# Scores in longer runs between fewer weighings, halved maxima of one reduction in four, and late value tiles spread

## The chip, the cores and the metric

One core of a Trainium2 chip. The time is the device time of one execution in microseconds; lower is better.

## The reference

Four sequences of 1024 tokens with 256 channels. A layer norm, attention with 16 heads of 16 dimensions and rotary positions, a layer norm and a residual; then a layer norm, a mixture of 8 experts (each token goes to 2), a layer norm and a residual. What matters here is the attention:

```python
q = (x @ Wq.T + bq).reshape(B, T, H, D)   # k, v alike; q and k rotated
scores = jnp.einsum('bthd,bshd->bhts', q, k) / np.sqrt(D)
attn = jax.nn.softmax(scores, axis=-1)
out = jnp.einsum('bhts,bshd->bthd', attn, v).reshape(B, T, C)
```

The softmax of this kernel subtracts a row maximum, which has to be known before the exponentials, as the scores that are exponentiated have keys on the partitions.

## The kernel before

Each engine runs its own program, in the order in which it is written; counting semaphores join them. There is no scheduler: an instruction whose wait isn't met holds up all behind it on its engine.

**Setup.** ScalarE turns the q and k weights' columns into the order that the rotation wants (`w_turn`, `b_turn`), copies the four halves of the cosine and sine tables out of PSUM and the bias columns `b_c`. Then it normalises the first 512 tokens. TensorE turns the tables, then the bias columns, then the first tokens (`turn_x(0)`), and projects (`project`). VectorE applies the rotation (`rope_unit`), GpSimd a part of it, ScalarE splits the result in a high and a low part, and SyncE stores these and loads them again as "stacks", three of which hold q and k of a group of four heads each.

**Groups.** There are 16 groups of 4 heads (`NG`), a group in 16 units (`UNITS`). In one unit the loop does two things on TensorE. For a later group, it computes the scores of 128 queries against all 1024 keys for two heads (`max_scores`: head `a` in two halves of 512 keys, to banks 4, 5 for `a` = 0 and 6, 7 for `a` = 1); VectorE reduces both banks of a head in one instruction to a row maximum (`reduce_max`). For the present group, it computes the transposed scores of 128 keys against 512 queries for four heads (`scores`, three banks in turn), which ScalarE exponentiates into `pt`. A maximum beside a score is called a pair here; they use different rows of the array. The maxima run `LEAD` = 5 units ahead of a group's end.

**Weighing.** `weigh` multiplies the exponentials of the unit two before (`LAG`) with the values: four heads side by side in the columns of the array, into bank 3. It does this in two parts of 256 queries, one after every second pair. Twice a group the sum in bank 3 is complete, and ScalarE copies it out (`save_o`, line 1356); the first weighing of the next half waits for that.

**Maxima.** After 8 units of maxima GpSimd splits them in two parts (`split_max`), VectorE turns them (`turn`), and SyncE brings them into the stack by way of memory. GpSimd also copies the values of a later group (`copy_values`) and, in groups 9 and 13, scales the output of a batch (`norm_o`), all in one queue.

**Ahead of the loop.** The maxima of group 0 and of the first 5 units of group 1 are computed without scores beside them. Of the 16 value tiles (`project_v`), 4 are done with the projections, and the other 12 follow one by one behind the maxima of the first 12 units. The loop waits until all are saved.

## Time and profile before

| | us |
|---|---|
| median of the runs shown | 1600.58 |
| the runs | 1593.86, 1600.58, 1622.9 |
| the profiled execution | 1592.43 |
| its span in the profile | 1590.5 |

| engine | busy us | share of the span |
|---|---|---|
| TensorE (PE) | 1446.7 | 91% |
| VectorE (DVE) | 1107.6 | 70% |
| ScalarE (ACT) | 852.3 | 54% |
| GpSimd (POOL) | 427.4 | 27% |

A time of the profile is counted from the span's start. PE are matmuls, PEld the loads of their stationary operand, and a matmul record's end is modelled. The stages that the change touches lie in the first half: setup and projections up to 98, maxima ahead of the loop up to 155, the loop up to 811. Output projection and experts follow.

### The profile page before, as it was taken

How to read it: one execution, taken by the hardware profiler on the slowest of the kernel's cores; microseconds unless marked ns; L12 is line 12 of the kernel's file. 1: busy time of each engine (PE TensorE's matmuls, PEld its weight loads, DVE VectorE, ACT ScalarE, POOL GpSimd, SP SyncE). 2: the span in 40 equal slices, each digit the busy share in tenths (PEclk: the TensorE clock that was granted, in tenths of full speed). 3: DMA queues.
4: the chain of work that ended last, by engine and by line, in shares of the span. 5: the costliest groups of instructions: out<-in, count | busy, mean ns of one | idle time of the engine just before them, and what ended most of it. 6: DMA issues, size and time to landing. Idle time of an engine off the chain costs nothing.

```text
span 1590.5 us, 29998 instructions
## 1 busy us (share of the span) xinstructions
PE 1446.7 (91%) x9435; PEld 800.9 (50%) x9436; DVE 1107.6 (70%) x1978; ACT 852.3 (54%) x1624; POOL 427.4 (27%) x411
## 2 busy tenths in 40 slices
PE   7989999999999999999999438999999999999950
PEld 4444333333333333333355226777777777777740
DVE  5989899999999989999026774555555555455525
ACT  5531788888888878888865321222222222222215
POOL 3760000000000010001014143444444444444425
PEclk9997899999999999999999759999999999999985
DMA  5887146334545554550429623222212222121136
GB/s 171 241 254 129 44 98 169 65 71 81 88 82 89 100 88 64 82 89 16 158 54 213 225 98 91 33 33 33 31 32 33 33 33 33 33 33 31 32 85 199
DMA packets 125116, 141.80 MB, mean 89 GB/s; under 512 B 55131, under 2 KB 98949, under 8 KB 125030
## 3 DMA queue, kind: packets, MB, share of 16 engines
q1 hardware_dynamic: 109126, 121.98, 33.2%
q0 software_dynamic: 15904, 18.66, 7.2%
q8 instruction: 56, 0.92, 0.2%
q14 instruction: 30, 0.25, 0.1%
HBM read 86.30 MB, written 54.30 MB: 88 GB/s over the span
## 4 chain that ended last, share of the span: by engine, by line
PE 78%; DVE 7%; issue 5%; ACT 4%; DMA 2%; SPq 2%; POOL 1%; DVEq 0%; POOLq 0%; ACTq 0%
PE psum L1681 20%; PE psum L1528 18%; PE psum L1554 16%; PE psum L1700 11%; PE psum L1691 3%; PE psum L1509 2%; PE psum L1540 2%; PE psum L1612 1%; PE psum L1493 1%; ACT work L1346 1%; DVE mx L942 1%; ACT weights L1356 1%; PE psum L1667 1%; PE psum L1610 1%; DVE work L1141 1%
## 5 line engine op out<-in xcount | busy, mean ns | idle before, releaser
L942 DVE TENSOR_REDUCE mx<-psum 128x1 f32<-128x1024 f32 x512 | 622.9, 1222 | 29.2 <-PE psum L1528 26.3
L1346 ACT ACTIVATE work<-psum 128x512 f32<-128x512 f32 x1024 | 556.7, 597 | 106.1 <-PE psum L1540 43.8
L1528 PE MATMUL psum<-stack 48*128 48x512 f32 x1024 | 379.3, 457 | 6.7 <-DVE mx L942 6.0
L1540 PE MATMUL psum<-stack 50*128 50x512 f32 x1024 | 379.1, 450 | 0.0
L1681 PE MATMUL psum<-weights,values 128*128 x1136 | 341.1, 454 | 0.6 <-DVE values L1161 0.6
L1554 PE MATMUL psum<-work,values 128*32 128x256 f32 x4096 | 330.5, 395 | 9.2 <-ACT weights L1356 9.2
L1528 PEld LDWEIGHTS psum<-stack 48*128 48x128 f32 x1024 | 154.2, 191 | 221.7 <-DVE mx L942 184.7
L1681 PEld LDWEIGHTS psum<-weights,values 128*128 128x128 f32 x1136 | 211.8, 192 | 99.2 <-issue 3.1
L1423 ACT ACTIVATE values<-values 128x342 f32<-128x342 f32 x142 | 69.3, 488 | 250.1 <-DVE values L1173 250.1
L1700 PE MATMUL psum<-weights,work 114*128 (+1 forms) x852 | 198.7, 383 | 1.3 <-ACT work L1434 0.8
L1554 PEld LDWEIGHTS psum<-work,values 128*32 128x32 f32 x4096 | 82.5, 108 | 198.2 <-ACT work L1346 100.5
L1700 PEld LDWEIGHTS psum<-weights,work 114*128 114x128 f32 (+1 forms) x852 | 158.0, 192 | 21.3 <-issue 1.8
L1540 PEld LDWEIGHTS psum<-stack 50*128 50x128 f32 x1024 | 153.8, 188 | 17.3 <-ACT work L1346 17.3
L829 POOL DMA_INDIRECT values<-xn_d,at_x x71 | 70.0, 986 | 280.9 <-DVE at_w L1204 275.5
L1429 ACT ACTIVATE work<-psum,dots 128x256 f32<-128x256 f32 x71 | 33.6, 473 | 201.3 <-PE psum L1700 196.7
L1173 DVE TENSOR_TENSOR values<-psum,work 128x342 f32<-128x342 f32 x142 | 73.1, 515 | 92.0 <-PE psum L1681 68.1
L836 POOL DMA_INDIRECT y_d<-work,at_y x71 | 115.2, 1622 | 39.7 <-issue 27.2
L1176 DVE TENSOR_TENSOR values<-psum,work 128x342 f32<-128x342 f32 x142 | 73.1, 515 | 62.2 <-PE psum L1681 62.2
L1192 DVE COPY work<-psum 114x256 f32<-114x256 f32 x71 | 30.2, 425 | 118.2 <-PE psum L1691 118.2
L753 POOL CAST m<-mx 128x16 fp32r<-128x16 f32 x32 | 6.3, 197 | 376.4 <-DVE mx L942 376.4
L1181 DVE TENSOR_TENSOR values<-values 128x342 f32<-128x342 f32 x142 | 73.3, 516 | 14.7
L744 POOL TENSOR_TENSOR values<-weights,dots 128x512 f32<-128x512 f32 x16 | 20.5, 1283 | 225.4 <-issue 225.2
(184 smaller groups left out, 1190.6 us busy)
## 6 DMA issues: line engine op xcount, KB each, us to landing
stack<-qk_scr SPq DMA_DIRECT2D x192, 128.0 KB, 6.1
qk_scr<-weights SPq DMA_DIRECT2D x16, 1024.0 KB, 4.8
weights<-in_w SPq DMA_DIRECT2D x8, 1368.0 KB, 7.1
ot_scr<-weights SPq DMA_DIRECT2D x16, 512.0 KB, 3.2
weights<-in_w SPq DMA_DIRECT2D x8, 684.0 KB
work<-in_b SPq DMA_DIRECT2D x8, 684.0 KB, 8.8
y_d<-zeros SPq DMA_DIRECT2D x1, 4224.0 KB, 14.3
v_scr<-weights SPq DMA_DIRECT2D x32, 128.0 KB, 2.5
```

The costliest lines, as they stand in the source:

```text
L829: pool.indirect_dma_start(out=x_row, out_offset=None, in_=xn2_d, in_offset=bass.IndirectOffsetOnAxis(ap=at_x[:, 0:1], axis=0)).then_inc(s_ ...
L836: pool.indirect_dma_start(out=y_d, out_offset=bass.IndirectOffsetOnAxis(ap=at_y[:, 0:1], axis=0), in_=y_row, in_offset=None, compute_op=AL ...
L942: dve.tensor_reduce(mx[:, r, a, t:t + 1], bank(4 + 2 * a, 2), AX, ALU.max, negate=True).then_inc(s_max, 1)
L1173: dve.tensor_tensor(gates[c], bank(2 * c)[:, 0:CH], bias(0), ALU.add).then_inc(s_gb, 1)
L1176: dve.tensor_tensor(hid[:, CH * c:CH * (c + 1)], bank(2 * c + 1)[:, 0:CH], bias(HID), ALU.add).then_inc(s_ub, 1)
L1181: dve.tensor_tensor(hid[:, CH * c:CH * (c + 1)], hid[:, CH * c:CH * (c + 1)], gates[c], ALU.mult).then_inc(s_hid, 1)
L1346: act.activation(pt[u % 4][:, j, :], bank((c + HG * u + n) % 3), ACT.Exp, scale=SC).then_inc(s_exp, 1)
L1528: ins = pe.matmul(bank(4 + 2 * a + half), qs[t3][at:at + QROWS, r, P * t:P * (t + 1)], ks[t3][at:at + QROWS, r, 512 * half:512 * (half + 1 ...
L1540: pe.matmul(bank((t3 + HG * u + n) % 3), ks[t3][at:at + MROWS, r, P * st:P * (st + 1)], qs[t3][at:at + MROWS, r, 512 * half:512 * (half + ...
L1554: last = pe.matmul(bank(3)[32 * j:32 * (j + 1), at:at + 256], vg[p][:, st, j, :], pt[u % 4][:, j, at:at + 256], start=st + part == 0, stop ...
L1681: last = pe.matmul(dst, x_t[:, k, :], w1_sb[:, bass.ds(e, 1), k, col:col + CH].rearrange("p a n -> p (a n)"), start=k == 0, stop=k == KC - 1)
L1700: last = pe.matmul(bank(7)[:, 0:C], h_t[0:rows, k, :], w2_sb[0:rows, bass.ds(e, 1), k, :].rearrange("p a n -> p (a n)"), start=k == 0, sto ...
```

## The change

Between two weighings stand runs of three, three and two pairs, where there were two: `weigh` now takes any stretch of queries, and `weigh_pieces` gives per two units 384 queries, 128 of the same unit with 256 of the next one, and 256. Of an even unit the second head's maximum so falls on both sides of a weighing, and VectorE reduces its two halves by themselves (`mx_b` holds the second ones); `join_max` takes the smaller of the two negated values every 8 units, and GpSimd waits for that. `maxima` counts five reductions in two units. `LEAD` becomes 6. The 12 late value tiles are spread over the 16 + 6 units of maxima ahead of the loop, and SyncE's loads of the first maxima are put between its stores of values accordingly. In the setup, GpSimd reorders the weights in place of ScalarE, VectorE copies the tables and the bias columns, and TensorE turns the bias columns after the first tokens.

```diff
--- before.py
+++ after.py
@@ -35,7 +35,7 @@
 EARLY_V = 2
 UNITS = 2 * ST
 BLOCKS = HG * UNITS
-LEAD = 5
+LEAD = 6
 LAG = 2
 SC = D ** -0.5
 CH = HID // 2
@@ -88,6 +88,12 @@
 
     for g in range(NG):
         body(0, g)
+
+
+def maxima(g, m, a, half):
+
+    before = 5 * (UNITS * g + m) // 2 + m % 2
+    return before + (a + 1 if m % 2 or a == 0 else 2 + half)
 
 
 def settle(eng, passed):
@@ -584,9 +592,8 @@
             load_stacks(sp, 0, 1)
             for m in range(EARLY_V, NB):
                 store_v(sp, m)
-                if m == 5:
-                    load_max_rows(sp, 0, 0, 0)
-            load_max_rows(sp, 0, 0, 1)
+                if m in (3, 5):
+                    load_max_rows(sp, 0, 0, (m - 3) // 2)
             sp.wait_ge(s_ones, 3)
             load_stacks(sp, 0, 2)
             for parts_of in s_pst:
@@ -714,6 +721,15 @@
                 pool.wait_ge(s_pad, n + 1)
             pool.memset(cent_t[:, :, :], 0.0).then_inc(s_pad, 1)
 
+            pool.wait_ge(s_wqkv, 32)
+            for k in range(KC):
+                for i in range(2):
+                    pool.tensor_copy(w_turn[:, k, i, :, :].rearrange("p s (d h) -> p s d h", h=H),
+                                     w_qkv[:, k, C * i:C * (i + 1)].rearrange("p (h s d) -> p s d h", s=2, d=HALF)).then_inc(s_wp, 1)
+            for i in range(2):
+                pool.tensor_copy(b_turn[0:1, i, :, :].rearrange("p s (d h) -> p s d h", h=H),
+                                 b_row[0:1, C * i:C * (i + 1)].rearrange("p (h s d) -> p s d h", s=2, d=HALF)).then_inc(s_wp, 1)
+
             def rotate(w):
 
                 p = w % 2
@@ -747,7 +763,7 @@
             def split_max(g, r):
 
                 at = PAIRS * g + r
-                pool.wait_ge(s_max, 2 * UNITS * g + UNITS * (r + 1))
+                pool.wait_ge(s_cmb, at + 1)
                 after(pool, s_m2t, at)
                 settle(pool, passed_pool)
                 pool.tensor_copy(m2[:, :, 0, :], mx[:, r, :, :]).then_inc(s_mh, 1)
@@ -923,6 +939,11 @@
             stats(0)
             spread_tables()
             invert(0)
+            for n, (table, at) in enumerate(((cos_t, 0), (cos_t, 512), (sin_t, 0), (sin_t, 512))):
+                dve.wait_ge(s_tab, n + 1)
+                dve.tensor_copy(table[:, at:at + 512], bank(n)).then_inc(s_tabs, 1)
+            dve.wait_ge(s_bt, 1)
+            dve.tensor_copy(b_c[:, :], bank(6)[:, 0:4]).then_inc(s_bc, 1)
             stats(1)
             invert(1)
             for m in range(NB):
@@ -936,10 +957,21 @@
             def reduce_max(g, m, a):
 
                 r, t = m // ST, m % ST
-                dve.wait_ge(s_mp, 2 * (UNITS * g + m) + a + 1)
                 if t == 0 and a == 0:
                     after(dve, s_m2, PAIRS * (g - 1) + r + 1)
+                if m % 2 == 0 and a == 1:
+                    for half, dst in enumerate((mx[:, r, a, t:t + 1], mx_b[:, r, t // 2:t // 2 + 1])):
+                        dve.wait_ge(s_mp, maxima(g, m, a, half))
+                        dve.tensor_reduce(dst, bank(4 + 2 * a + half), AX, ALU.max, negate=True).then_inc(s_max, 1)
+                    return
+                dve.wait_ge(s_mp, maxima(g, m, a, 1))
                 dve.tensor_reduce(mx[:, r, a, t:t + 1], bank(4 + 2 * a, 2), AX, ALU.max, negate=True).then_inc(s_max, 1)
+
+            def join_max(g, r):
+
+                dve.wait_ge(s_max, maxima(g, ST * r + ST - 1, 1, 1))
+                both = mx[:, r, 1, :].rearrange("p (t s) -> p t s", s=2)[:, :, 0]
+                dve.tensor_tensor(both, both, mx_b[:, r, :], ALU.min).then_inc(s_cmb, 1)
 
             def turn(g, r):
 
@@ -956,6 +988,8 @@
                     if m == ST:
                         turn(g, 0)
                     reduce_max(g, m, 1)
+                    if m % ST == ST - 1:
+                        join_max(g, m // ST)
 
             def invert_sums(b):
 
@@ -1301,21 +1335,6 @@
                 act.activation(hl[w % 4][:, 0, :, :].bitcast(F32R), rr[w % 2], ACT.Copy).then_inc(s_hi, 1)
 
             deviation(0)
-            act.wait_ge(s_wqkv, 32)
-            for k in range(KC):
-                for i in range(2):
-                    act.activation(w_turn[:, k, i, :, :].rearrange("p s (d h) -> p s d h", h=H),
-                                   w_qkv[:, k, C * i:C * (i + 1)].rearrange("p (h s d) -> p s d h", s=2, d=HALF),
-                                   ACT.Copy).then_inc(s_wp, 1)
-            for i in range(2):
-                act.activation(b_turn[0:1, i, :, :].rearrange("p s (d h) -> p s d h", h=H),
-                               b_row[0:1, C * i:C * (i + 1)].rearrange("p (h s d) -> p s d h", s=2, d=HALF),
-                               ACT.Copy).then_inc(s_wp, 1)
-            for n, (table, at) in enumerate(((cos_t, 0), (cos_t, 512), (sin_t, 0), (sin_t, 512))):
-                act.wait_ge(s_tab, n + 1)
-                act.activation(table[:, at:at + 512], bank(n), ACT.Copy).then_inc(s_tabs, 1)
-            act.wait_ge(s_bt, 1)
-            act.activation(b_c[:, :], bank(6)[:, 0:4], ACT.Copy).then_inc(s_bc, 1)
             normalise(0)
             save_xt(0)
             deviation(1)
@@ -1468,12 +1487,6 @@
                     src = spread[n // 2][:, 4 * (n % 2) + a, :, :].rearrange("p d h -> p (d h)")
                     last = pe.transpose(bank(n)[:, P * a:P * (a + 1)], src, ident[:, :])
                 last.then_inc(s_tab, 1)
-            pe.wait_ge(s_wp, 6)
-            for i in range(2):
-                for s in range(2):
-                    last = pe.matmul(bank(6)[:, 2 * i + s:2 * i + s + 1], b_turn[0:1, i, s, :], ones_f[0:1, 0:1], start=True, stop=True)
-            last.then_inc(s_bt, 1)
-
             def turn_x(m):
                 pe.wait_ge(s_xn, TB * (m + 1))
                 for k in range(KC):
@@ -1511,6 +1524,12 @@
                 last.then_inc(s_vp, 1)
 
             turn_x(0)
+            pe.wait_ge(s_wp, 6)
+            for i in range(2):
+                for s in range(2):
+                    last = pe.matmul(bank(6)[:, 2 * i + s:2 * i + s + 1], b_turn[0:1, i, s, :], ones_f[0:1, 0:1], start=True, stop=True)
+            last.then_inc(s_bt, 1)
+
             for m in range(NB):
                 project(2 * m)
                 if m + 1 < NB:
@@ -1523,11 +1542,11 @@
             def max_scores(g, t3, m, a, half):
 
                 r, t, at = m // ST, m % ST, 64 * a
-                if half == 0:
-                    after(pe, s_max, 2 * (UNITS * g + m) + a - 1)
+                if half == 0 and (g, m) != (0, 0):
+                    pe.wait_ge(s_max, maxima(g, m - 1, a, 1) if m else maxima(g - 1, UNITS - 1, a, 1))
                 ins = pe.matmul(bank(4 + 2 * a + half), qs[t3][at:at + QROWS, r, P * t:P * (t + 1)],
                                 ks[t3][at:at + QROWS, r, 512 * half:512 * (half + 1)], start=True, stop=True)
-                if half == 1:
+                if half == 1 or (m % 2 == 0 and a == 1):
                     ins.then_inc(s_mp, 1)
 
             def scores(g, t3, u, n):
@@ -1540,22 +1559,31 @@
                 pe.matmul(bank((t3 + HG * u + n) % 3), ks[t3][at:at + MROWS, r, P * st:P * (st + 1)],
                           qs[t3][at:at + MROWS, r, 512 * half:512 * (half + 1)], start=True, stop=True).then_inc(s_sp, 1)
 
-            def weigh(g, p, u, part):
+            def weigh(g, p, u, lo, hi):
 
                 half, st = u // ST, u % ST
-                if part == 0:
+                if lo == 0:
                     pe.wait_ge(s_exp, BLOCKS * g + HG * (u + 1))
                     if st == 0:
                         if half == 0:
                             pe.wait_ge(s_vg, g + 1)
                         after(pe, s_oe, 2 * g + half)
-                at = 256 * part
                 for j in range(HG):
-                    last = pe.matmul(bank(3)[32 * j:32 * (j + 1), at:at + 256], vg[p][:, st, j, :],
-                                     pt[u % 4][:, j, at:at + 256], start=st + part == 0, stop=st + part == ST,
+                    last = pe.matmul(bank(3)[32 * j:32 * (j + 1), lo:hi], vg[p][:, st, j, :],
+                                     pt[u % 4][:, j, lo:hi], start=st + lo == 0, stop=(st, hi) == (ST - 1, 512),
                                      tile_position=(0, 32 * j))
-                if part == 1:
+                if hi == 512:
                     last.then_inc(s_pv, 1)
+
+            def weigh_pieces(g, p, u, n):
+
+                pieces = {(0, 2): ((0, 0, 384),), (1, 1): ((0, 384, 512), (1, 0, 256)), (1, 3): ((1, 256, 512),)}
+                first = u // 2 * 2 - LAG
+                if first < 0:
+                    g, p, first = g - 1, 1 - p, first + UNITS
+                if g >= 0:
+                    for step, lo, hi in pieces.get((u % 2, n), ()):
+                        weigh(g, p, first + step, lo, hi)
 
             def group(i, c):
                 g, p, t3 = over(i, c, 1), c % 2, c % 3
@@ -1569,11 +1597,7 @@
                         if more:
                             max_scores(g + ahead, (c + ahead) % 3, m, n // 2, n % 2)
                         scores(g, t3, u, n)
-                        if n % 2 == 1:
-                            if u >= LAG:
-                                weigh(g, p, u - LAG, n // 2)
-                            elif c > 0:
-                                weigh(g - 1, 1 - p, UNITS + u - LAG, n // 2)
+                        weigh_pieces(g, p, u, n)
 
             pe.wait_ge(s_xt, 2 * NB)
             pe.wait_ge(s_va, 2 * EARLY_V)
@@ -1582,24 +1606,24 @@
                 for m in range([UNITS, LEAD][g]):
                     for n in range(HG):
                         max_scores(g, g, m, n // 2, n % 2)
-                    b = 2 * EARLY_V + m
-                    if g == 0 and b < 2 * NB:
-                        if m == 0:
-                            pe.wait_ge(s_r1, NU)
-                            pe.wait_ge(s_x1, NU)
-                        project_v(b // 2, b % 2)
+                    unit = UNITS * g + m
+                    late = 2 * (NB - EARLY_V)
+                    if unit == 0:
+                        pe.wait_ge(s_r1, NU)
+                        pe.wait_ge(s_x1, NU)
+                    for b in range(late * unit // (UNITS + LEAD), late * (unit + 1) // (UNITS + LEAD)):
+                        project_v(EARLY_V + b // 2, b % 2)
             pe.wait_ge(s_va, 2 * NB)
             pe.wait_ge(s_pad, 2)
             groups(pe, group)
             for u in range(UNITS - LAG, UNITS):
-                for part in range(2):
-                    weigh(NG - 1, 1, u, part)
+                weigh(NG - 1, 1, u, 0, 512)
 
 
             pe.wait_ge(s_wo, 48)
             pe.wait_ge(s_oe, 2 * NG)
             pe.wait_ge(s_exp, BLOCKS * NG)
-            pe.wait_ge(s_max, 2 * UNITS * NG)
+            pe.wait_ge(s_max, maxima(NG - 1, UNITS - 1, 1, 1))
 
             def project_o(u):
                 pe.wait_ge(s_div, 2 * (u // 4) + u % 4 // 2 + 1)
```

## Rows read from the trace of the kernel before

**Rows 1.** The chain that ended last, by engine, from the page

```profile
PE 78%; DVE 7%; issue 5%; ACT 4%; DMA 2%; SPq 2%; POOL 1%; DVEq 0%; POOLq 0%; ACTq 0%
```

**Rows 2.** Timeline of TensorE, last group and its end (start us, us)

```profile
761.55 0.73 PE L1540 MATMUL psum<-stack 50*128 50x512 f32 x2
...
762.78 0.73 PE L1540 MATMUL psum<-stack 50*128 50x512 f32 x2
...
808.43 2.37 PE L1554 MATMUL psum<-work,values 128*32 128x256 f32 x40
```

**Rows 3.** Timeline of TensorE in the loop, around a saved bank

```profile
305.96 0.49 PE L1528 MATMUL psum<-stack 48*128 48x512 f32 x1
...
306.30 0.39 PE L1528 MATMUL psum<-stack 48*128 48x512 f32 x1
...
306.99 0.64 PE L1554 MATMUL psum<-work,values 128*32 128x256 f32 x8 [0.30 <-ACT weights L1356]
...
307.56 0.50 PE L1528 MATMUL psum<-stack 48*128 48x512 f32 x1
```

**Rows 4.** Timeline of VectorE in the loop, the last row at half clock

```profile
288.27 2.46 DVE L942 TENSOR_REDUCE mx<-psum 128x1 f32<-128x1024 f32 x2 [0.38 <-PE psum L1528]
...
290.77 17.18 DVE L942 TENSOR_REDUCE mx<-psum 128x1 f32<-128x1024 f32 x14
308.33 2.46 DVE L942 TENSOR_REDUCE mx<-psum 128x1 f32<-128x1024 f32 x2 [0.38 <-PE psum L1528]
...
582.00 1.23 DVE L942 TENSOR_REDUCE mx<-psum 128x1 f32<-128x1024 f32 x1 [0.93 <-PE psum L1528]
```

**Rows 5.** Timeline ahead of the loop, with value tiles, and the loop's first pair

```profile
98.36 2.35 DVE L942 TENSOR_REDUCE mx<-psum 128x1 f32<-128x1024 f32 x2
...
107.70 0.74 PE L1528 MATMUL psum<-stack 48*128 48x512 f32 x4
...
108.47 2.36 DVE L942 TENSOR_REDUCE mx<-psum 128x1 f32<-128x1024 f32 x2 [0.82 <-PE psum L1528]
...
110.29 1.31 PE L1528 MATMUL psum<-stack 48*128 48x512 f32 x4
...
113.46 0.74 PE L1528 MATMUL psum<-stack 48*128 48x512 f32 x4
...
155.36 0.79 PE L1540 MATMUL psum<-stack 50*128 50x512 f32 x1
```

**Rows 6.** Timeline ahead of the loop, without value tiles

```profile
134.20 9.50 DVE L942 TENSOR_REDUCE mx<-psum 128x1 f32<-128x1024 f32 x8 [0.33 <-PE psum L1528]
...
135.48 0.73 PE L1528 MATMUL psum<-stack 48*128 48x512 f32 x2 [0.83 <-DVE mx L942]
```

**Rows 7.** Timeline of the setup

```profile
7.45 3.65 PE L1469 MATMUL psum<-ident,work 128*128 128x128 f32 x16 [7.45 <-DVE work L897]
...
9.12 2.23 ACT L1307 ACTIVATE work<-work 128x256 f32<-128x256 f32 x4 [0.72 <-DMA work<-in_bqkv]
...
14.42 2.06 ACT L1281 ACTIVATE work<-weights,work 128x256 f32<-128x256 f32 x4
...
19.18 5.61 PE L1493 MATMUL psum<-weights,work 128*128 128x512 f32 x8 [0.69 <-ACT weights L1287]
```

**Rows 8.** Timeline of GpSimd and of VectorE at group 10's start

```profile
568.45 4.72 POOL L774 TENSOR_TENSOR weights<-weights 128x1024 f32<-128x1024 f32 x2
...
573.65 0.21 DVE L948 STREAM_TRANSPOSE m_t<-m 128x32 f32<-128x32 f32 x1 [1.88 <-POOL m L755]
```

**Rows 9.** Stretches: length, PE busy (records), granted clock as a share, DMA share, GB/s

```profile
136.00:140.00 4.00, 2.69 (x7) 0.89 0.98 215
...
156.00:172.00 16.00, 15.70 (x80) 0.50 0.31 47
...
576.00:584.00 8.00, 8.00 (x56) 0.57 0.88 121
...
742.00:746.00 4.00, 4.00 (x44) 1.00 0.04 8
```

2 lines of the change are left out of this document (added).

## The prediction

> **What bounds the kernel now.** I read the chain that ended last first: TensorE holds 78% of it [rows 1]. Then I read the timelines of the stages which the diff touches, and asked of each which wait ends last.
>
> In the attention loop a slot (two pairs of a maximum beside a score, then a weighing of 256 queries) costs TensorE 0.34 us to the second pair (306.30 - 305.96), 0.57 us from the weighing to the next pair (307.56 - 306.99) and 0.32 us between these two, the rest of 1.23 [rows 3]. In the last group, where no maxima are left and VectorE is idle, the slot is still 1.23 us [rows 2]. So TensorE sets this loop, though its waits are put down to VectorE: the released semaphore had long been there. VectorE's fourteen reductions of a stretch lie 1.23 us apart [rows 4], but left alone it starts one every 1.13 us, although each record is 1.22 us long, because the end of one overlaps the start of the next [rows 6]. After a reduction's end TensorE follows within 0.06 us [rows 6]. One stall is left: twice per group the first weighing waits until ScalarE has saved the output bank [rows 3], and TensorE loses 306.99 - 306.62 = 0.37 us [rows 3]. Hence a half group is 16 x 1.23 + 0.37 = 20.06 us, which is the distance of the two stalls in VectorE's rows, 308.33 - 288.27 [rows 4].
>
> Ahead of the loop, group 0's maxima with twelve late value tiles run at 5.76 us for two units (107.70 to 113.46), with VectorE idle for 0.82 us there [rows 5]. Without value tiles (from 134.20) VectorE sets the pace at 2 x 1.13 us a unit [rows 6]. During this the granted clock falls to half and stays there through the first slots of the loop [rows 9].
>
> **Setup.** ScalarE loses the four weight reorderings, the bias, four table copies and the bias column: it normalised the first tile at 14.42 and could do so from 9.12 on, where the first of these copies stands, or earlier [rows 7]. What is late next is TensorE: it turns tables until 7.45 + 3.65 = 11.10 [rows 7]. At that row's 0.23 us a record, eight transposes of x take 1.9 us and the bias matmuls, now behind them, another 1.9 us: the first projection starts at 14.9 instead of 19.18. GpSimd was idle then. Six copies of 256 elements at the rate of its 128x1024 product (4.72 / 2 / 1024 = 2.3 ns an element [rows 8]) are 3.6 us, done at 12.7, under the transposes. At twice that price they would end at 16.3 and the gain would shrink to 1 us. VectorE gets the table copies and, worse, a wait for the bias columns, behind which the second tile's statistics queue: they end near 17, its normalised rows near 20, just when TensorE wants them. I take -4.0 us, bounds -1 and -5.
>
> **Ahead of the loop.** Twelve tiles now go over 22 units, one in every second unit but for two neighbours at the middle and the end. Take a unit followed by a tile. When TensorE issues its second head's maximum, VectorE holds at most the rest of one reduction and this one: 1.13 - 0.15 + 2 x 0.60 = 2.2 us of work (0.15 us: the overlap and the reply; a reduction of 512 is estimated at 0.60 us, namely 1.13 less 512 columns at 1024 / 1.067 us, that is, the same start cost as a whole one). TensorE comes back with data after 0.66 + 1.93 + 0.77 = 3.36 us (the pairs, the tile, 110.29 - 107.70 - 0.66, and 0.73 us for fresh scores with their semaphore) [rows 5]. That leaves a hole of 1.18 us, in every couple of units: 3 x 1.13 + 2 x 0.60 + 1.18 = 5.77 us. That is what two tiles in a couple cost before [rows 5]: spreading them hides nothing, as each one blocks TensorE's queue for longer than two buffers last. Eleven couples are 63.4 us. Before, 12 units at 2.88 and 9 at 2.26 us made 55; from the first reduction (98.36) to the loop (155.36) it was 57.0 [rows 5]. With the same edges the change adds 6.3 us, one unit of it (2.3 us) taken over from the loop, where it was free. I bound the term by +2 and +9.
>
> **The loop.** Per two units it has eight pairs as before and the same 1024 queries of weighing, but three switches instead of four. Weighings in a row take 0.43 us per 256 queries (the forty records at the end last 2.37 us [rows 2]; four weighings and the last one's record of 0.64 us: 1.73 / 4). A slot's 1.23 us less 2 pairs at about 0.235 and 0.43 leaves 0.33 us for a switch. TensorE alone would so need 4.92 - 0.33 = 4.59 us. VectorE needs 3 x 1.13 + 2 x 0.60 = 4.59 us. Both look like a gain of 7%. But a dependency joins them. The first pair of an even unit's second head (the third pair of its unit) waits for the whole reduction of the odd unit before it, in every two units, and that maximum is ready late: the last one is issued in the third run. Count from that pair at 0: its start after a wait and the way to the weighing 0.42; 384 queries and the switch 0.57 + 0.21 = 0.78; the fourth maximum and the next two 0.34 + 0.235; then 0.32 + 0.78; 0.34 to the odd unit's last pair: 3.22. Scores there after 0.39 + 0.04, the reduction 1.22, the reply 0.06: 4.93 us. The old period is 4.92. So the switch that is saved is spent waiting at this pair; that sum doesn't depend on how a run's third pair is spaced (0.21 to 0.34), since the pair after a wait pays what the other saves.
>
> What remains: the stall of the saved bank goes, since the first weighing now comes one pair later and lies under this wait. Its cover is the wait itself; were the wait gone, a few tenths would come back. Two joins a group cost VectorE about 0.3 us each (end of its reduction, an operation of 4 elements, no overlap), and 0.03 us of it appears. A half group becomes 19.75 instead of 20.06 us: -0.3 x 29 = -8.7 us. The last 22 units have no maxima, and there the saved switch counts: -2.8 us.
>
> GpSimd's queue takes some of it back. With a lead of six, the maxima of the first half are due one unit earlier, but in two groups the same 4.72 us of output scaling stand ahead of their splitting [rows 8]. VectorE waited 1.88 us there. It would now wait 1.88 + 2.46 + 0.3 = 4.65 us, and one period is paced by that: +2.8 us twice, and the save stall that it used to cover in part, +6.2 us in all. The ordinary value copy ends in time. Sum of the loop: -8.7 - 2.8 + 6.2 = -5.3 us, between -10 and +15; the upper bound is from the weighing of 128 queries. No row shows one. It may cost 0.21 us (half of 256) or as much as 256 does, 0.43 us, if loading its weights binds. I take the half, since the records of 256 queries hide their loads with time to spare, and 0.1 us more would already be +11 us.
>
> **The clock.** Before, eight slots in 155 to 173 took 2.16 us (582.00 less the reduction before it, 0.93 + 1.23) instead of 1.23 [rows 4, 9]: 7.5 us. It fell where TensorE had 67% records for 4 us [rows 9]. With tiles to the end its share ahead of the loop is some 80%, so I expect the loop to start at full clock: -7.5 us, bounds 0 and -7.5. The two waits for GpSimd go the other way. An equal wait made the clock fall once (7 us near half clock, 3.0 us lost) and once not [rows 9]. I expect that waits two and a half times as long make it fall both times: +3 us.
> The Trainium skill, in "TensorE: Matmul & The Clock Gate" under "Part 1: The HAM clock gate", says that the default state is the throttled one and that activity releases it, so a pause of TensorE is paid again afterwards. By that rule both waits cost a fall, where the rows alone would allow none; the sum would be 6 us lower without it.
>
> **Sum.** -4.0 + 6.3 - 5.3 - 7.5 + 3 = -7.5 us on the profiled execution's 1592.4 us (span 1590.5, 1.9 around it): 1585. That execution lies 8 us under the median of the three runs shown and 1.4 under their lowest; for a median of undisturbed runs I add 3 us: 1588 us.
>
> **The rivals.**
> *The dependency is not last* (0.12). Were the wait of the even unit's second head always met in time, half groups would be 18.7 us: 29 x 1.1 = 32 us less, 1556 us. For it: both engines' own sums are 4.59. Against it: the row of 1.22 us and the position of the last maximum leave no room.
> *The clock falls ahead of the loop* (0.2). The new mixture of short maxima and one tile in two units comes after a pause of 4 us at about 95. If it holds TensorE at half clock, a tile takes 1.93 x 2.16 / 1.23 = 3.4 us: 12 x 1.5 = 18 us, and the 7.5 us are not saved: 1613 us; half of it gives 1600. It decides from the point at which half clock lasts beyond the second tile. This is the case slower than before.
> *The weighing of 128 queries binds* (0.13): +0.1 to +0.21 us in each of some 120 couples, 1600 to 1612 us.
> *The setup gains nothing* (0.05), as GpSimd's reordering is slow: 1592 us.
> The forecast itself has 0.5, with its own range 1575 to 1597.
>
> **How the numbers follow.** The range 1564 to 1612 leaves out most of the first rival and the far end of the second and third. About 2% is what can be told from no change. Faster by over 2% (under 1569 against the median shown) is the first rival and the forecast's lower tail: 0.16. Slower by over 2% needs two of the slow cases at once: 0.07. The rest is 0.77.
>
> **What would show it.** Slots of the loop: a couple of units at 4.93 us with a wait of some 0.35 us at the third pair of even units, put down to the reduction. Reductions of 512 of about 0.69 us. No wait for the saved bank. The loop starting near 157.5 (161.7 less the setup's 4). A couple ahead of it at 5.77 us with holes of about 1.2 us in VectorE. The transposes in groups 10 and 14 waiting 4 to 5 us for GpSimd. The first projection at 15. I am wrong above all if a couple of units takes 4.6 us, or if the clock is at half before the loop.

## The result and the profile after

The changed kernel takes 1614.4 us in the median of four runs (1613.31 to 1615.6), the kernel before 1599.5 beside it. Each kernel has some longer executions with a lower granted clock over the whole span; the medians here include them, the ratios don't. The ratio is 1.0105 with a 95% interval of 1.0077 to 1.0134: slower by 1%, and the interval does not reach 1, which would be no difference. Predicted were 1588 us, with 1564 to 1612 as the range. The profiled execution took 1614.05 us, with a span of 1612.1; of before these were 1592.43 and 1590.5. Of the change's stages I name four events and take the distances between them.

| from | to | before, us | after, us | difference | predicted |
|---|---|---|---|---|---|
| start of the span | first reduction | 98.36 | 93.07 | -5.3 | -4.0 |
| first reduction | loop's first pair | 57.0 | 84.8 | +27.8 | +6.3 |
| loop's first pair | last saved bank | 655.5 | 656.3 | +0.8 | -9.8 |
| last saved bank | end | 779.6 | 777.9 | -1.7 | 0 |

The second row holds more than the whole difference. The timeline of the changed kernel there, TensorE and VectorE (start us, us), beside [rows 5]:

```profile
93.07 1.22 DVE L968 TENSOR_REDUCE mx<-psum 128x1 f32<-128x1024 f32 x1
...
96.68 3.78 PE L1522 MATMUL psum<-work,weights 128*128 128x256 f32 x8
101.64 1.23 DVE L968 TENSOR_REDUCE mx<-psum 128x1 f32<-128x1024 f32 x1 [3.64 <-PE psum L1547]
...
109.80 1.23 DVE L968 TENSOR_REDUCE mx<-psum 128x1 f32<-128x1024 f32 x1 [3.20 <-PE psum L1547]
...
117.25 1.22 DVE L968 TENSOR_REDUCE mx<-psum 128x1 f32<-128x1024 f32 x1 [2.69 <-PE psum L1547]
...
177.84 0.49 PE L1559 MATMUL psum<-stack 50*128 50x512 f32 x1
```

A couple of units takes 8.2 us (101.64 to 109.80) and then 7.5 us, where the prediction had 5.77. The first spread tile takes 3.78 us for its eight records (four products, two records each), twice the 1.93 us that I had worked out, and VectorE stands idle for 2.7 to 3.6 us behind each tile, not for 1.18. The stretches of the changed kernel say why (length, PE busy and records, granted clock, DMA share, GB/s):

```profile
100.00:110.00 10.00, 8.46 (x22) 0.54 0.84 205
110.00:120.00 10.00, 6.68 (x19) 0.80 0.98 141
120.00:130.00 10.00, 8.62 (x19) 0.50 0.25 54
130.00:140.00 10.00, 8.94 (x30) 0.84 0.25 56
...
150.00:160.00 10.00, 8.06 (x23) 0.67 0.26 56
160.00:170.00 10.00, 7.46 (x18) 0.64 0.12 27
```

A share between 0.5 and 1 is a mean over both levels, 1.2 and 2.4 GHz. The clock goes up and falls again through the whole stage, and some 55 of its 84.8 us run at the lower level. The records' busy share, 67 to 89%, looks like the 80% I had counted on. But at the lower level a record lasts about twice as long (the tile of 3.78 us), so this share says little; the section on the steps reads it where the clock was full.

In the loop, TensorE's timeline shows a couple of units around the wait that the change adds (the pair of L1547 at 301.68 is the third of an even unit):

```profile
300.87 0.49 PE L1547 MATMUL psum<-stack 48*128 48x512 f32 x1
...
301.20 0.39 PE L1547 MATMUL psum<-stack 48*128 48x512 f32 x1
...
301.68 0.50 PE L1547 MATMUL psum<-stack 48*128 48x512 f32 x1
...
302.18 0.85 PE L1572 MATMUL psum<-work,values 128*32 128x384 f32 x8
...
303.31 0.39 PE L1547 MATMUL psum<-stack 48*128 48x512 f32 x1
...
303.54 0.39 PE L1547 MATMUL psum<-stack 48*128 48x512 f32 x1
...
303.86 0.86 PE L1572 MATMUL psum<-work,values 128*32 128x128 f32 x16
```

A third pair that waits for nothing follows after 0.23 us (303.54 - 303.31); this one follows after 0.48 us, as VectorE's reduction isn't through. The weighing of 128 queries and the 256 of the next unit are one row of sixteen products, 303.86 to 304.65, as long as the one of 384 queries. A couple of units comes to 4.95 us where VectorE has nothing but reductions to do; with its joins and transpositions the mean is 5.03 (a quarter of 20.10, below). No row of a weighing is put down to the saved bank any more.

VectorE's joins and GpSimd's work beside them, timelines of both, and the transposition of group 11's first maxima, at group 10's start:

```profile
306.15 1.28 POOL L760 TENSOR_TENSOR values<-weights,dots 128x512 f32<-128x512 f32 x1 [18.48 <-issue]
...
306.67 0.78 DVE L974 TENSOR_TENSOR mx<-mx,mx_b 128x4 f32<-128x4 f32 x1
...
327.01 0.17 DVE L974 TENSOR_TENSOR mx<-mx,mx_b 128x4 f32<-128x4 f32 x1
...
589.51 4.68 POOL L790 TENSOR_TENSOR weights<-weights 128x1024 f32<-128x1024 f32 x2
...
594.66 0.21 DVE L980 STREAM_TRANSPOSE m_t<-m 128x32 f32<-128x32 f32 x1 [3.95 <-POOL m L771]
```

The same operation on four elements a partition takes 0.17 us, or 0.78 us when GpSimd's copy of a group's values lies over it. It then ends at 307.45, just behind that copy (306.15 + 1.28 = 307.43): the join waits until the copy is over. ScalarE's save of bank 3 gives the length of a half group (its timeline):

```profile
286.30 0.60 ACT L1375 ACTIVATE weights<-psum 128x512 f32<-128x512 f32 x1
306.16 0.60 ACT L1375 ACTIVATE weights<-psum 128x512 f32<-128x512 f32 x1
326.50 0.60 ACT L1375 ACTIVATE weights<-psum 128x512 f32<-128x512 f32 x1
```

Halves of 19.86 and 20.34 us alternate, 20.10 in the mean: the long ones hold the long join. Before, each was 20.05. The two that hold GpSimd's scaling are 25.80 and 25.92 us. In the last units, where no maxima are left, a half is 18.67 us instead of 20.04.

And of the setup, the timeline beside [rows 7]:

```profile
8.97 2.08 ACT L1315 ACTIVATE work<-weights,work 128x256 f32<-128x256 f32 x4 [0.44 <-DVE work L906]
9.06 2.31 POOL L727 COPY work<-work 128x256 f32<-128x256 f32 x4 [3.73 <-DMA work<-in_bqkv]
...
14.23 3.70 PE L1506 MATMUL psum<-weights,work 128*128 128x512 f32 x8
```

### The profile page after: what moved, and what is told of

It is laid out like the page before. It is cut to its first block, busy times and chain, and to the rows that moved or that the text cites. A ratio compares the mean times of both kernels' runs of the same rounds, so it can differ in the third digit from the quotient of the medians.

```text
span 1612.1 us, 30126 instructions
## 1 busy us (share of the span) xinstructions
PE 1449.6 (90%) x9419; PEld 823.6 (51%) x9420; DVE 1117.0 (69%) x2143; ACT 835.2 (52%) x1613; POOL 431.2 (27%) x417
## 4 chain that ended last, share of the span: by engine, by line
PE 68%; DVE 20%; issue 7%; DMA 1%; POOL 1%; ACT 1%; SPq 1%; DVEq 0%; POOLq 0%; ACTq 0%
PE psum L1705 20%; DVE mx L968 12%; PE psum L1724 11%; PE psum L1547 10%; PE psum L1572 10%; PE psum L1559 4%; PE psum L1522 3%; PE psum L1715 3%; PE psum L1636 2%; PE psum L1634 1%; DVE mx_b L965 1%; DVE mx L965 1%; PE psum L1506 1%; PE psum L1691 1%; PE psum L1655 1%
## 5 line engine op out<-in xcount | busy, mean ns | idle before, releaser
L1365 ACT ACTIVATE work<-psum 128x512 f32<-128x512 f32 x1024 | 544.4, 600 | 98.0 <-PE psum L1559 73.7
L968 DVE TENSOR_REDUCE mx<-psum 128x1 f32<-128x1024 f32 x384 | 465.4, 1220 | 46.2 <-PE psum L1547 36.9
L1547 PE MATMUL psum<-stack 48*128 48x512 f32 x1024 | 380.6, 459 | 39.8 <-DVE mx L968 20.0
L1547 PEld LDWEIGHTS psum<-stack 48*128 48x128 f32 x1024 | 161.6, 191 | 283.5 <-issue 122.8
L1572 PE MATMUL psum<-work,values 128*32 128x384 f32 x4080 | 303.5, 393 | 0.3
L1559 PEld LDWEIGHTS psum<-stack 50*128 50x128 f32 x1024 | 161.8, 187 | 26.6 <-ACT work L1365 21.1
L1572 PEld LDWEIGHTS psum<-work,values 128*32 128x32 f32 x4080 | 88.8, 109 | 125.9 <-issue 103.1
L965 DVE TENSOR_REDUCE mx_b<-psum 128x1 f32<-128x512 f32 x128 | 88.0, 688 | 2.3 <-PE psum L1547 1.5
## 6 DMA issues: line engine op xcount, KB each, us to landing
y_d<-zeros SPq DMA_DIRECT2D x1, 4224.0 KB, 14.9
```

The costliest lines, as they stand in the source:

```text
L965: dve.tensor_reduce(dst, bank(4 + 2 * a + half), AX, ALU.max, negate=True).then_inc(s_max, 1)
L968: dve.tensor_reduce(mx[:, r, a, t:t + 1], bank(4 + 2 * a, 2), AX, ALU.max, negate=True).then_inc(s_max, 1)
L1365: act.activation(pt[u % 4][:, j, :], bank((c + HG * u + n) % 3), ACT.Exp, scale=SC).then_inc(s_exp, 1)
L1547: ins = pe.matmul(bank(4 + 2 * a + half), qs[t3][at:at + QROWS, r, P * t:P * (t + 1)], ks[t3][at:at + QROWS, r, 512 * half:512 * (half + 1 ...
L1559: pe.matmul(bank((t3 + HG * u + n) % 3), ks[t3][at:at + MROWS, r, P * st:P * (st + 1)], qs[t3][at:at + MROWS, r, 512 * half:512 * (half + ...
L1572: last = pe.matmul(bank(3)[32 * j:32 * (j + 1), lo:hi], vg[p][:, st, j, :], pt[u % 4][:, j, lo:hi], start=st + lo == 0, stop=(st, hi) == ( ...
```

## The experiments

All are timed beside runs of the kernel before; a ratio is to those. Spans and events are of the profiled execution. The kernels were timed in three batches (e1 to e4, e5 to e8, e9 to e12), in which the kernel before had medians of 1608.6, 1600.5 and 1607.9 us. So where two kernels of different batches are compared, their spans stand beside the difference.

**Which part costs the time.** Three kernels take the change apart. The first is the changed kernel with the value tiles where they were, and with SyncE's loads as they were:

```diff
-                    for b in range(late * unit // (UNITS + LEAD), late * (unit + 1) // (UNITS + LEAD)):
-                        project_v(EARLY_V + b // 2, b % 2)
+                    b = 2 * EARLY_V + m
+                    if g == 0 and b < 2 * NB:
...
+                        project_v(b // 2, b % 2)
```

> The changed kernel with its late value tiles back behind the first twelve units, one each, and SyncE's loads of the first maxima back in their old places; all else stays. Theory (the spread tiles empty VectorE's two buffers in every couple of units and thin TensorE's work so far that it runs at half clock): the loop starts some 58 to 60 us after the first reduction instead of 85, and the time falls by about 25 us, to 1587 to 1592 us. Rival (the earlier setup or the clock by itself makes this stage long, wherever the tiles stand): the stage stays above 75 us and the time above 1603 us.

Measured: 1594.1 us, ratio 0.9957 (0.9906 to 1.0008). The span is 22 us shorter than the changed kernel's (1590.0 against 1612.1). The stage from the first reduction to the loop takes 60.3 us (92.31 to 152.62) instead of 84.8, and the clock is 1.0 from 100 to 130.

The second is the kernel before with the new setup alone, GpSimd and VectorE taking ScalarE's copies and TensorE turning the bias columns later:

```diff
+            pool.wait_ge(s_wqkv, 32)
+            for k in range(KC):
+                for i in range(2):
+                    pool.tensor_copy(w_turn[:, k, i, :, :].rearrange("p s (d h) -> p s d h", h=H),
...
-            act.wait_ge(s_wqkv, 32)
```

> The kernel before with the setup part alone (GpSimd reorders the weights, VectorE copies tables and bias columns, TensorE turns the bias columns after the first tokens). Theory: the 5.3 us that the first reduction came earlier in the changed kernel reach the end: 5 us faster than before. Rival (the gain is lost again to a longer pause of TensorE ahead of the maxima, or to the clock): within 2 us of before, or slower.

Measured: 1587.5 us, ratio 0.9916 (0.9864 to 0.9967). The first reduction stands at 92.28, 6.1 us earlier than before, and the span is 4.6 us shorter (1585.9). That is all that the first kernel has over before: with longer runs and old tiles, its 1594.1 isn't under this one.

The third is the kernel before with the spread tiles and SyncE's loads alone (21 units, as `LEAD` is 5):

```diff
-                    b = 2 * EARLY_V + m
-                    if g == 0 and b < 2 * NB:
...
+                    for b in range(late * unit // (UNITS + LEAD), late * (unit + 1) // (UNITS + LEAD)):
+                        project_v(EARLY_V + b // 2, b % 2)
```

> The kernel before with its twelve value tiles spread over its 21 units of maxima and nothing else. Theory: the spread by itself costs the 28 us that the stage grew by in the changed kernel, less the one unit that is not in it: 20 to 26 us slower than before (1613 to 1620 us). Rival (the spread is only harmful together with the halved maxima and the lead of six): less than 8 us slower, the 6 us of the empty buffers at full clock.

Measured: 1626.8 us, ratio 1.0123 (0.9986 to 1.0261), an interval that includes no difference. The profiled execution, at 1643, is 14 us longer than the next of the four, at a granted clock of 0.919 over its span against 0.930 to 0.941, and it lost 17 us behind the last saved bank, where nothing is changed. Its stage is 78.1 us (97.35 to 175.45), 21 more than before, at a granted clock of 0.50 to 0.92 in all stretches. This points to the spread costing the time by itself, without the shortened reductions, but such an execution doesn't show it. For the changed kernel the first of the three kernels does: with the tiles put back its stage is 24.5 us shorter. SyncE's loads, which moved with the tiles, aren't the cause, as a later kernel leaves them in their new places and has a stage of 57.5 us.

**Is it the clock, or the blocked queue?** A spread tile holds up TensorE's queue whatever the clock is. To part the two, the next kernel leaves everything in place and adds work without use: one product of 512 columns in each unit ahead of the loop that has no tile, but for the first.

```diff
+            def fill(b):
+                pe.wait_ge(s_va, b - 3)
+                pe.matmul(bank((b - 2 * EARLY_V) % 4), xn_t[:, 2, 0, 0:P], w_qkv[:, 0, 0:512], start=True, stop=True)
...
+                    mine = late * unit // (UNITS + LEAD), late * (unit + 1) // (UNITS + LEAD)
+                    if unit > 0 and mine[0] == mine[1] and mine[0] < late:
+                        fill(2 * EARLY_V + mine[0])
```

> The changed kernel with one useless matrix product more (128 rows, 512 columns, fp32, some 0.9 us at full clock) in each of the ten units ahead of the loop that have no value tile, written to the bank that the next tile overwrites: nothing is left out, work is added. Theory (the holes of the spread stage are as long as they are because TensorE runs at half clock there, and it does so because the spread left it idle too often): with more work the clock is granted for most of the stage and the loop starts 63 to 70 us after the first reduction instead of 85; the time falls by 10 to 20 us. Rival (the stage is long by its order alone, the clock only follows): the stage takes 85 us or more, and the time rises by up to 9 us.

Measured: 1599.3 us, ratio 1.0007 (0.9973 to 1.0041), 15 us under the changed kernel with more to compute (spans of 1597.4 and 1612.1). The useless products are nine, not the ten of the expectation. The stage takes 67.6 us (91.54 to 159.11). Its stretches, as above:

```profile
90.00:100.00 10.00, 7.10 (x16) 0.54 0.56 211
100.00:110.00 10.00, 8.95 (x30) 0.95 0.91 195
110.00:120.00 10.00, 8.63 (x31) 1.00 0.96 153
120.00:130.00 10.00, 9.83 (x30) 0.83 0.26 55
130.00:140.00 10.00, 9.27 (x35) 1.00 0.10 22
```

The clock falls at the first tile here too (0.54), but then it is back and stays. VectorE's timeline in this kernel:

```profile
100.12 1.23 DVE L968 TENSOR_REDUCE mx<-psum 128x1 f32<-128x1024 f32 x1 [3.63 <-PE psum L1551]
...
105.95 1.23 DVE L968 TENSOR_REDUCE mx<-psum 128x1 f32<-128x1024 f32 x1 [1.15 <-PE psum L1551]
...
111.78 1.22 DVE L968 TENSOR_REDUCE mx<-psum 128x1 f32<-128x1024 f32 x1 [1.15 <-PE psum L1551]
```

At full clock a couple is 5.83 us with a hole of 1.15 us. I had worked out 5.77 and 1.18. So both theories are right in part, and their shares can be read roughly: the blocked queue gives 67.6 instead of the 60.3 us of the tiles as before, and the half clock the remaining 17.2 us up to 84.8. The 17.2 are rather too small for the clock, since the stage with the filler still has two falls and carries the useless work.

**Would smaller pieces do?** If blocking is the cost of a spread tile, quarters of it between the maxima should hide it. The kernel cuts each late tile into its four products and spreads these, one or two at a time, over 20 of the 22 units:

```diff
+            def quarter_v(b, q):
+                m, half, a, k = b // 2, b % 2, q // 2, q % 2
+                t = 2 * half + a
...
+                        if n % 2:
+                            h = 2 * unit + n // 2 - 2
+                            for q in range(max(0, QUARTERS * h // HALVES), min(QUARTERS, max(0, QUARTERS * (h + 1) // HALVES))):
+                                quarter_v(2 * EARLY_V + q // 4, q % 4)
```

> The changed kernel with each late value tile cut into its four matrix products, which are spread one or two behind each head's maxima, over 20 of the 22 units. Theory (a whole tile blocks TensorE for longer than VectorE's two buffers last; a quarter, 0.5 us, doesn't): VectorE runs nearly without holes, the loop starts 52 to 56 us after the first reduction, TensorE is busy and its clock full, and the time is 30 to 35 us under the changed kernel's, 1580 to 1585 us. Rival (pieces of 0.5 us at every switch cost as much as they hide): the stage takes 60 us or more and the time is 1590 us or above.

Measured: 1635.9 us, ratio 1.0208 (1.0113 to 1.0303). My expectation fell altogether; the rival's bounds were met, but not for its reason, the cost of the switches. The stage takes 102.8 us (92.76 to 195.54). Its stretches and TensorE's timeline:

```profile
100.00:110.00 10.00, 10.00 (x19) 0.50 0.85 199
...
180.00:190.00 10.00, 10.00 (x19) 0.50 0.14 32
```
```profile
144.65 1.22 PE L1533 MATMUL psum<-work,weights 128*128 128x256 f32 x2
145.80 1.22 PE L1559 MATMUL psum<-stack 48*128 48x512 f32 x2
146.95 1.22 PE L1533 MATMUL psum<-work,weights 128*128 128x256 f32 x2
148.10 1.22 PE L1559 MATMUL psum<-stack 48*128 48x512 f32 x2
```

TensorE's records leave no gap for 90 us (100 to 190), VectorE waits for it, and the clock never leaves the lower level. So "keep TensorE busy and the clock stays up", which the filler seemed to say, isn't the whole of it. A kernel with the same quarters and the first two mends of the loop told below (both heads halved, scaling moved) shows it again, with a stage of 102.8 us and the loop from 194.42:

> e7_both_split_scale_later with the quartered value tiles of e6_quarter_tiles. Theory (the three losses are independent): the loop starts 52 to 56 us after the first reduction at full clock instead of 58 at half, 8 to 12 us less than e7_both_split_scale_later, 1544 to 1549 us. Rival (with the odd units' maxima halved too, VectorE is the bound ahead of the loop, and the halved clock at its start comes back): within 3 us of e7_both_split_scale_later.

Measured: 1599.1 us, ratio 0.9977 (0.9937 to 1.0017); the clock is 0.50 in each stretch of the stage, and it is 44 us behind the kernel with these mends and the tiles as before.

One more kernel leaves the first four late tiles whole, one a unit, and quarters only the other eight (with all three mends of the loop):

```diff
+            WHOLE = 4
+            QUARTERS, HALVES = 8 * (NB - EARLY_V) - 4 * WHOLE, 2 * (UNITS + LEAD - WHOLE) - 4
...
+                    if unit < WHOLE:
+                        project_v(EARLY_V + unit // 2, unit % 2)
```

> e9_copy_later with the first four late value tiles whole, one in each of the first four units, and the other eight in quarters over the remaining units. e6_quarter_tiles ran its whole stage at half clock with TensorE busy all the time. Theory A (a stage in quarters keeps the clock that it starts with; what held e6 at half was the pause ahead of its first tile, which whole tiles overcome): full clock after the first tiles, the loop starts 53 to 55 us after the first reduction, and the time is 5 to 12 us under e9_copy_later's. Theory B (short pieces between two maxima lose the clock by themselves): half clock comes back in the quartered part and the time is 15 to 30 us above e9_copy_later's.

Measured: 1560.2 us, ratio 0.9754 (0.9657 to 0.9851). Its stretches:

```profile
90.00:100.00 10.00, 7.97 (x30) 0.83 0.59 219
100.00:110.00 10.00, 10.00 (x36) 1.00 0.88 191
110.00:120.00 10.00, 10.00 (x33) 1.00 1.03 164
120.00:130.00 10.00, 10.00 (x32) 1.00 0.56 122
130.00:140.00 10.00, 10.00 (x32) 1.00 0.02 2
```

Quarters run at full clock here, behind whole tiles that ran at it. They kept the clock that they found, and in the kernel with quarters alone they didn't bring it back. Which property of the whole tiles, or of the start of the stage, decides this isn't shown. The stage takes 57.5 us (91.89 to 149.41), no less than the 57.8 us of the old order with the same loop (below), so the 5 to 12 us that I expected weren't there. The median is even 14 us above that kernel's: four of the six runs took 1560 to 1562 us and the profiled one 1543.87, which is as fast as that kernel. No profile of a long run was kept, so where they lose the time is open.

**Is the loop's dependency what holds it?** The prediction says that the whole reduction of an odd unit binds, not the engines' sums. In the next kernel (tiles as before) the second head's maximum of odd units, too, is reduced in halves, and its bank waits for the half alone:

```diff
-                if m % 2 == 0 and a == 1:
-                    for half, dst in enumerate((mx[:, r, a, t:t + 1], mx_b[:, r, t // 2:t // 2 + 1])):
+                if a == 1:
+                    for half, dst in enumerate((mx[:, r, a, t:t + 1], mx_b[:, r, t:t + 1])):
...
-                if half == 0 and (g, m) != (0, 0):
-                    pe.wait_ge(s_max, maxima(g, m - 1, a, 1) if m else maxima(g - 1, UNITS - 1, a, 1))
+                if (half == 0 or a == 1) and (g, m) != (0, 0):
+                    pe.wait_ge(s_max, maxima(g, m - 1, a, half if a else 1) if m else maxima(g - 1, UNITS - 1, a, half if a else 1))
```

> As e1_tiles_as_before, and the second head's maximum is reduced in halves in odd units too, so that each half of the bank pair is free by itself; the pair that waited for the odd unit's whole reduction now waits for its first half. VectorE gets 0.06 us more work in two units, 4.65 us. Theory (that wait is what sets 4.95 us for two units): 4.7 us for two units, a half group 19.1 to 19.3 instead of 20.1 us, 25 to 30 us faster than e1_tiles_as_before. Rival (TensorE's pairs and switches, or VectorE's work, set the 4.95 us): two units stay at 4.9 to 5.0 us and the time within 4 us of e1_tiles_as_before.

Measured: 1570.1 us, ratio 0.9823 (0.9688 to 0.9958), 24 us under the first kernel of this section, in the same batch. Halves are 19.67 and 19.07 us, 19.37 in the mean, and from the loop's first pair to the last saved bank it is 637.2 us instead of 660.3. VectorE has one start cost more per two units and the loop is still faster: it was the chain of waits, not VectorE's sum.

**GpSimd's queue.** In the next kernel the scaling `norm_o` moves from groups 9 and 13 behind the first `split_max` of groups 10 and 14; in the one after it the copy of the values moves behind the first `split_max` too:

```diff
-                if not (isinstance(g, int) and g + 2 >= NG):
-                    copy_values(i, c + 2)
-                if g in (9, 13):
-                    norm_o((g - 9) // 4)
+                        if r == 0 and g > 0:
+                            copy_values(i, c + 1)
+                        if r == 0 and g in (10, 14):
+                            norm_o((g - 10) // 4)
```

> As e4_both_split, with GpSimd's scaling of two batches' outputs (4.7 us each) moved from ahead of the splitting of groups 11's and 15's first maxima to behind it. Theory (this scaling holds the splitting up, VectorE's transpose and then TensorE wait for it, and TensorE's clock falls after the pause): the two long half groups of e4_both_split, 27.5 and 26.1 us, become 19.1 to 19.7, and the time falls by 12 to 15 us, to 1555 to 1558 us. Rival (the two half groups are long for another reason, such as transfers of the same groups): less than 3 us.

Measured with `norm_o` alone moved: 1555.1 us, ratio 0.9684 (0.961 to 0.9758), 15 us under the one before (spans of 1553.7 and 1567.4). The two halves that wait for the scaling, 27.46 and 26.05 us with both heads halved, became 19.67: 14.2 us.

> e7_both_split_scale_later with GpSimd's copy of a group's values (1.28 us) moved from ahead of the splitting of the next group's first maxima to behind it. In the changed kernel the join of the halved maxima (four elements a row, 0.16 us) took 0.78 us where it met this copy, and the half groups alternate between 19.87 and 20.34 us. Theory (VectorE's join, both inputs in SBUF, is held up by GpSimd's copy, and the delay goes through to TensorE): the half groups become alike, 19.1 us instead of 19.07 and 19.66, and the time falls by 14 x 0.5 = 7 us. Rival (the longer half group is the transpose and the wait for the splitting, with or without the copy): the half groups still alternate, within 2 us.

Measured with both moved: 1545.9 us, ratio 0.9666 (0.9569 to 0.9763), another 9 us (spans of 1542.9 and 1553.7). All joins are 0.17 us now, and the halves (ScalarE's timeline) no longer alternate:

```profile
597.68 0.60 ACT L1375 ACTIVATE weights<-psum 128x512 f32<-128x512 f32 x1
616.76 0.60 ACT L1375 ACTIVATE weights<-psum 128x512 f32<-128x512 f32 x1
635.83 0.60 ACT L1375 ACTIVATE weights<-psum 128x512 f32<-128x512 f32 x1
```

This is the fastest version: 19.07 us a half, and 3.3% under the kernel before.

**Does filling help there too?** The fastest version with the same useless product in its tile-less units ahead of the loop, where the clock falls to 0.50 from 130 to 150:

> e9_copy_later with one useless product (128 rows, 512 columns, 0.9 us at full clock) behind the maxima of each unit ahead of the loop that has no value tile, but for the last. Theory (VectorE sets the pace there with 2.3 us a unit, TensorE idles and falls to half clock, which it still has in the loop's first slots): the clock stays full, the stage is no longer and the loop's first slots are short: 3 to 6 us less than e9_copy_later. Rival (the clock doesn't follow such filler, or the filler delays the maxima): no gain, or up to 5 us more.

Measured: 1554.3 us, ratio 0.9737 (0.9602 to 0.9872), an interval that overlaps the last one. Two of the four runs took 1544 us, the profiled one among them, and two 1565; the four runs of the fastest version took 1544.85 to 1548.77. The clock stays at 1.0 up to 150 and falls to 0.66 in the next 10 us, at the loop's start. The last bank is saved at 764.33 instead of 765.09. Postponing the fall gained under 1 us, which no time here resolves, instead of the 3 to 6 us expected.

**Are the longer runs needed?** The kernel before with setup, scaling and copy mended, but its runs of two pairs, whole reductions and `LEAD` 5:

> The kernel before (runs of two pairs, whole maxima, a lead of five, tiles in the first twelve units) with three parts alone: the new setup, the scaling and the value copy behind the splitting. Against e9_copy_later it has the old loop. Theory (longer runs pay only once the odd units' maxima are halved too, and then by 0.9 us a half group and 3 us at the end): 1578 to 1583 us, 27 to 33 us above e9_copy_later. Rival (the gain of e4 and e7 came from elsewhere than the runs): within 10 us of e9_copy_later.

Measured: 1583.0 us, ratio 0.9887 (0.9787 to 0.9987), 37 us above the fastest. Its halves are 20.05 us, and the loop up to the last saved bank takes 651.1 us instead of 615.1. The longer runs with halved reductions of all second heads are worth 36 us there. The longer runs alone, with the prediction's one reduction in four halved, were worth nothing: 660.3 us of the first kernel against 658.8 of the setup alone. Halved reductions with the old runs weren't tried. They had little to give, as the old runs need 20.03 us for a half even in the last units, where there are no maxima.

## Why the prediction was wrong, by its steps

**Setup**, -4.0: it came to -5.3. GpSimd's four copies took 2.31 us, 0.58 each where I had put 0.60, and the first projection started at 14.23, not 14.9. VectorE did wait 2.38 us for the bias columns (until 14.34) with the second tile's statistics behind them, and TensorE then 1.06 us for that tile's rows, at 18.99 where I had put 20. The term was right but 1.3 us small.

**Ahead of the loop**, +6.3 at full clock: the working holds, as far as a kernel with filler in it can tell. That gives a couple of 5.83 us and a hole of 1.15 us. Its stage of 67.6 us is 10.6 above before, not 6.3: 11 couples are 64.1, the rest is the clock's fall at the first tile and one in 120 to 130. The 0.60 us for a reduction of 512 came as estimated (94.20 to 94.80 in VectorE's rows); its 1.067 us for 1024 columns stands in no row, but the two measured sizes, 1.13 and 0.60 us, give 1.06. The row in [rows 6] from which I read 1.13 us is a mean of 1.18 over eight reductions; 1.13 is what the two at 98.36 in [rows 5] give (2.35 - 1.22).

**The clock**, -7.5 and +3: the step that failed. I wrote: "With tiles to the end its share ahead of the loop is some 80%, so I expect the loop to start at full clock". No row gives 80%. By [rows 5] a couple of units at full clock has one tile (1.93 us) and two units of maxima (0.66 us each when nothing holds them, 1.31 with a wait inside): 3.3 to 3.9 of its 5.77 us, or 56 to 68%. The 80% are VectorE's share there, 4.59 of 5.77 us. The stretches of the changed kernel's stage with full clock throughout bear this out (length, PE busy and records, granted clock, DMA share, GB/s):

```profile
109.20:112.50 3.30, 1.53 (x7) 1.00 1.01 128
116.00:119.30 3.30, 1.94 (x9) 1.00 1.06 183
133.10:139.80 6.70, 5.63 (x22) 1.00 0.35 77
143.30:146.60 3.30, 1.57 (x7) 1.00 0.00 0
150.10:153.50 3.40, 1.88 (x9) 1.00 0.38 83
167.20:170.50 3.30, 1.58 (x7) 1.00 0.51 114
174.00:177.80 3.80, 3.15 (x15) 1.00 0.00 0
```

TensorE is busy for 17.3 of these 27.1 us, 64%. That is no more than the 67% ahead of the fall before [rows 9], from which I had argued; the 81% from 100 to 180 are raised by records that half clock made longer. With the filler the share at full clock is 87 and 90% (17.82 of 20.40 us from 101, 30.73 of 34.10 us from 125), and the clock stays. So the rows at hand warned of the fall, and I used a wrong share.

The rival "the clock falls ahead of the loop", to which I gave 0.2 with 1613 us, is what happened. Its working had 3.4 us for each of twelve tiles, 18 us in all. Ten of the twelve took 3.33 to 3.78 us, and together they are 16.3 us over ten of 1.99; the filler puts the clock at 17.2 us of the stage. The loop's start is at half clock too: its first half group took 28.05 us instead of 30.56, -2.5 and not -7.5. Of +3 for the two long waits, both falls came: 0.58 in 594 to 602 and 0.57 in 760 to 768.

In the changed kernel's stretches the clock comes and goes (0.54, 0.80, 0.50, 0.84), while TensorE's pauses from 100 on last 1.4 us at most and are waits for VectorE. The Trainium skill, in "TensorE: Matmul & The Clock Gate" under "HAM oscillation — how this bites in real kernels", describes a kernel that waits for a transfer in every round and starts each round at the lower clock again. The trace agrees with the page in the to and fro, not in the kind of wait. The quarters' 90 us at 0.50 with no gap between records aren't explained by it.

**The loop's dependency**: right. A couple took 4.95 us where I had 4.93. The rival in which it isn't last (0.12) didn't happen, and halving the odd units' reduction as well gave 24 of the 32 us that the rival had promised.

**The half group**, -8.7 us: the second step that failed, in size. I had 19.75 us and it is 20.10, so the term became +1.5. The short halves are 0.11 above me, with the join at 0.17 us. The long ones carry 0.48 more, as the join lies under GpSimd's copy; moving the copy took it away. In the prediction I let the value copy "end in time" for what waits for it, and didn't ask what its running does to VectorE. The Trainium skill, in "GPSIMD Engine Reference" under "Specifications", says that GpSimd and VectorE share their interfaces to SBUF, with contention when VectorE's operation has two operands there. The join is such an operation, and the trace agrees: the join ended when the copy did. The reduction beside the scaling (589.50), which reads PSUM, kept its 1.21 us.

**The last 22 units**, -2.8: the last three halves are 3.8 us shorter. **GpSimd's scaling**, +6.2: the transposition waited 3.95 us, between "4 to 5" and the 1.88 of before. The two halves are 25.80 and 25.92 instead of 24.57 and 21.62: +5.5 us, with the clock's falls in it that I had counted apart. **The weighing of 128 queries** costs nothing beyond its share: 384 queries in two pieces take what they take in one. **The saved bank's stall** went, under the wait, as said.

These make +1.5 - 3.8 + 5.5 - 2.5 = +0.7 in the loop, against +0.8 measured.

## What to carry to other kernels

Ask of each stage that leaves TensorE small pauses what the clock does there, and price it at both levels. Work out TensorE's busy share from rows at full clock, as records at half clock are longer and hide the pauses. Work that is spread out for balance can cost more through the clock than it hides, here some 17 of 28 us. Where two engines alternate over a few buffers, the sums of both can be under the period while a chain through one late, whole operation sets it; splitting that operation pays even if it costs its engine another start. Order a helper engine's queue by who waits for each item, and look also at which instructions of other engines its own will meet: two moves in GpSimd's queue brought 24 us here.

## What the runs showed of the hardware

TensorE ran for 90 us at 1.2 GHz with no gap between its records, when products of 256 columns over 128 rows took turns in pairs with pairs of 512 columns over 48 rows. Nearly the same mixture ran at 2.4 GHz for 40 us after four whole tiles. I can't say which property of whole tiles brings the clock up, and matmul ends are modelled, so short gaps may be hidden in those records.

One useless product in each but the first of the units without a tile, nine in all, made the kernel 15 us faster.

A VectorE operation of 4 elements a partition with two operands in SBUF took 0.17 us, and 0.78 us where GpSimd's operation of 512 elements (1.28 us, the copy of the values) was under way; it ended 0.02 us behind that one's end. A reduction out of PSUM that lies under GpSimd's scaling of 4.68 us (589.50) kept its 1.21 us.
